# First self-attention's outputs stored head by head from SBUF, and divided by the softmax sums in the dense stage after it

## The reference, cut to what matters

```python
h1 = _ln(x, n1_g, n1_b)
q = (h1 @ q1).reshape(b, n, 20, 16).transpose(0, 2, 1, 3)     # k, v alike
sim = jnp.einsum('bhid,bhjd->bhij', q, k) * 16 ** -0.5
a = jax.nn.softmax(sim, axis=-1)
out = jnp.einsum('bhij,bhjd->bhid', a, v)
out = out.transpose(0, 2, 1, 3).reshape(b, n, 320)
x = out @ o1_w + o1_b + x
h2 = _ln(x, n2_g, n2_b)
q = h2 @ q2                                                   # queries of the cross-attention
```

## Time and profile before

| | |
|---|---|
| median of 3 runs | 3340.49 us (3337.49 to 3342.36) |
| the profiled execution | 3342.7 us, its span 3341.0 us |
| PE busy | 2936.9 us, 88% |
| DVE busy | 2157.7 us, 65% |
| ACT busy | 1892.4 us, 57% |
| POOL busy | 805.5 us, 24% |

### The profile page before, as it was taken

How to read it: one execution, slowest core, us unless ns; L and a number is a source line. 1 busy time by engine, 2 the same in 40 slices (tenths; PEclk the granted TensorE clock), 3 DMA queues, 4 the chain that set the end, 5 groups by cost and what they waited for, 6 DMA issues and landing times. The chain is left out here.

```text
span 3341.0 us, 47964 instructions
## 1 busy us (share of the span) xinstructions
PE 2936.9 (88%) x15594; PEld 1775.7 (53%) x15594; DVE 2157.7 (65%) x3834; ACT 1892.4 (57%) x3214; POOL 805.5 (24%) x1149
## 2 busy tenths in 40 slices
PE   6989999978696999998959999879978577899999
PEld 5754444457455888886731111111126342788888
DVE  5668888837453444444649999968868685444443
ACT  4328888844353232233549999989975355333322
POOL 2021221114640000000027888200003471200000
PEclk9969999989798999998975555555559898899999
DMA  8663333336762000001567557266723213010000
GB/s 228 211 166 101 106 107 103 90 80 158 165 176 46 10 10 19 9 0 38 152 173 163 128 137 164 32 90 83 97 56 96 79 45 92 26 36 18 25 17 16
DMA packets 358243, 296.57 MB, mean 89 GB/s; under 512 B 175602, under 2 KB 281914, under 8 KB 358058
## 3 DMA queue, kind: packets, MB, share of 16 engines
q1 hardware_dynamic: 347994, 273.93, 34.0%
q0 software_dynamic: 7280, 18.07, 2.1%
q10 hardware_dynamic: 2784, 2.29, 0.4%
HBM read 177.53 MB, written 114.52 MB: 87 GB/s over the span
## 5 line engine op out<-in xcount | busy, mean ns | idle before, releaser
L1591 PE MATMUL nat<-k_stack,q_stack 48*128 48x512 bf16 x640 | 381.0, 605 | 71.5 <-DMA k_stack<-k1w 31.1
L1391 DVE TENSOR_REDUCE neg_max<-nat 128x1 f32<-128x512 f32 x640 | 400.7, 682 | 61.3 <-PE nat L1250 61.2
L1625 DVE TENSOR_REDUCE m_all<-nat 128x1 f32<-128x512 f32 x640 | 423.3, 691 | 18.1 <-PE nat L1591 17.8
L804 POOL TENSOR_TENSOR rstd<-var_eps,neghalf 128x4 f32<-128x4 f32 x48 | 51.9, 1081 | 1588.0 <-DVE var_eps L1028 1588.0
L1645 ACT ACTIVATE nat<-nat,m_all 128x512 f32<-128x512 f32 x640 | 427.7, 2130 | 3.0 <-DVE m_all L1625 2.9
L1645 ACT ACTIVATION_READ_ACCUMULATOR nat<-nat,m_all 128x1 f32 x640 | 403.6, 1674 | 0.0
L1054 DVE SCALAR_TENSOR_TENSOR ff<-outp,bias,gel 128x512 f32<-128x512 f32 x160 | 120.1, 751 | 417.6 <-PE outp L326 417.6
L1325 ACT ACTIVATE probs<-sT 128x1024 f32<-128x1024 f32 x320 | 328.0, 1027 | 93.1 <-PE sT L1259 85.5
L968 ACT ACTIVATE gel<-outp,bias 128x512 f32<-128x512 f32 x160 | 110.0, 688 | 351.6 <-PE outp L326 351.6
L1839 ACT ACTIVATE exps<-sT 128x1024 f32<-128x1024 f32 x320 | 293.4, 1573 | 10.5 <-PE sT L1788 10.5
L972 ACT CAST ff_hi<-ff 128x512 fp32r<-128x512 f32 x160 | 99.2, 620 | 312.3 <-DVE ff L1054 312.3
(11 more groups left out here) (561 smaller groups left out, 7163.3 us busy)
## 6 DMA issues: line engine op xcount, KB each, us to landing
v<-vpad SPq DMA_DIRECT2D x64, 320.0 KB, 2.8
q_stack<-q_part SPq DMA_DIRECT2D x90, 160.0 KB, 5.8
k_stack<-k1w SPq DMA_DIRECT2D x90, 160.0 KB, 10.5
q_stack<-q_hi SPq DMA_DIRECT2D x160, 64.0 KB, 2.5
v_stack<-v SPq DMA_DIRECT2D x40, 256.0 KB, 3.2
q_stack<-q_hi SPq DMA_DIRECT2D x80, 128.0 KB, 2.8
raw<-v SPq DMA_DIRECT2D x16, 640.0 KB, 14.9
k_stack<-k_hi SPq DMA_DIRECT2D x158, 64.0 KB, 2.2
```

Source lines behind the costliest of these rows:

```text
L1391: dve.tensor_reduce(neg_max[:, n % 2, qt, 2 * pr + ab:2 * pr + ab + 1], nat[(16 * (n + 2) + t) % 3][:, :], AX.X, ALU.max, negate=True).the ...
L1591: pe.matmul(bank[i % NAT][:, :], q_stack[half, slot, g, pr, qt * P:(qt + 1) * P], k_stack[half, slot, g, pr, :], start=True, stop=True).th ...
L1625: dve.tensor_reduce(k.m_all[:, column(i // TILES, i % TILES)], bank[i % NAT][:, :], AX.X, ALU.max, negate=True).then_inc(s["e_max_ready"], 1)
```

## The change

**In the attention.** The outputs are no longer turned, normalised and stored by token. `turn_output` on PE, the copy `o_turned` on ACT, the reciprocal of each quad on DVE and `norm` on POOL are gone. ACT copies `o_ps` into one of two buffers `o_sb[:, n % 2]`, and POOL stores them as they are (`store`, L1379 to L1385): one DMA for the four rows of sums and one for each head's 16 rows, five a quad. POOL does this for quad m-5 in its pass m, behind the parts. ACT's copy waits for `b_o_stored{n % 2}`, that is for all five stores of the quad which last used its buffer. Once per sample SP loads the 20 rows of sums (`load_sums`), DVE inverts them (`invert`), POOL splits the result in a high and a low part (`split_shares`), SP stores both.

**In the dense stage.** It runs by feature. The `oT` transposes are gone; instead PE spreads the inverted sums of a sample to the features (`scale`, three matmuls of a 40-row matrix `spread` with the 40 rows `shares`), and DVE multiplies the loaded outputs by them in place, ahead of the split. The three steps stand behind `("stats", 0)` and are taken two samples ahead. SP loads the outputs in 3 DMAs and the shares in one.

```diff
+        scale = [("scale", m) for m in range(3)] if recips is not None else []
...
+            if scale:
+                ahead["scale"] = 2
+            body = [("stats", 0), *scale, *oT[0:2], items[0], oT[2], ("norm", 0), items[1], items[2], oproj[0], ("double", 0),
                     zT[0], zT[1], oproj[1], zT[2], oproj[2], oproj[3]]
...
                 def load_attn_T(b, split_b=None):
                     if split_b is not None:
                         sp.wait_ge(s["oT_split"], at["oT_split"] + split_b * 3 + 3)
+                    if scale:
+                        sp.dma_start(words(shares[:, :]), rows(recips, b * (2 * HEADS), 2 * HEADS)
+                                     ).then_inc(s["attn_in_loaded"], 16)
...
+                    if kind == "scale":
+                        if isinstance(b, int) and b + m == 0:
+                            pe.wait_ge(s["spread_set"], at["spread_set"] + 1)
+                        if m == 0:
+                            pe.wait_ge(s["attn_in_loaded"],
+                                       at["attn_in_loaded"] + b * (16 * n_attn) + 16 * n_attn)
+                        bank_free(pe, st, b)
+                        pe.matmul(bank_of(st, r)[:, :], spread[:, m * P:(m + 1) * P], shares[:, :], start=True, stop=True
+                                  ).then_inc(s[turned[st][0] + "_full"], 1)
+                    elif kind == "oT" and not by_feature:
...
+                    if kind == "scale":
+                        if m == 0:
+                            dve.wait_ge(s["attn_in_loaded"],
+                                        at["attn_in_loaded"] + b * (16 * n_attn) + 16 * n_attn)
+                        bank_full(dve, st, b)
+                        dve.tensor_tensor(attn[:, m, :], attn[:, m, :], bank_of(st, r)[:, :], ALU.mult
+                                          ).then_inc(s[turned[st][0] + "_drained"], 1)
...
+                def load_sums(b):
+                    for r in range(2):
+                        wait(sp, f"b_o_stored{r}", 80 * ((QUADS * (b + 1) - r + 1) // 2))
+                    sp.dma_start(sums, rows(sums_dram, b * HEADS, HEADS).rearrange("h (x t) -> h x t", t=P)
+                                 ).then_inc(s["a_sums_loaded"], 16)
+
+                def store_shares(b):
+                    wait(sp, "a_share_split", 2 * b + 2)
+                    for i, half in enumerate((share_hi, share_lo)):
+                        sp.dma_start(rows(recips, (2 * b + i) * HEADS, HEADS).rearrange("h (x t) -> h x t", t=P),
+                                     words(half)).then_inc(s["a_recip_stored"], 16)
...
+                    if exists(n - 4) and (n - 4) % QUADS == QUADS - 1:
+                        load_sums((n - 4) // QUADS)
+                    if exists(n - 7) and (n - 7) % QUADS == QUADS - 1:
+                        store_shares((n - 7) // QUADS)
...
-                def turn_output(n):
-                    wait(pe, "a_o_copied", n + 1)
-                    wait(pe, "a_turn_free", output_use(n) - 1)
-                    for qt in range(TT):
-                        mm = pe.transpose(output_bank(n)[:, qt * P:(qt + 1) * P], o_sb[:, qt * P:(qt + 1) * P],
-                                          k.ident[:, :])
-                    mm.then_inc(s["a_turn_full"], 1)
...
                         wait(act, "a_pv_done", n - 1)
-                        wait(act, "a_turn_full", output_use(n - 3) + 1 if n > 2 else 0)
-                        act.copy(o_sb[:, :], o_ps[:, :]).then_inc(s["a_o_copied"], 1)
+                        wait(act, f"b_o_stored{n % 2}", 80 * (n // 2 - 1))
+                        act.copy(o_sb[:, n % 2, :], o_ps[:, :]).then_inc(s["a_o_copied"], 1)
...
-                        if exists(n - 2) and j == 2:
-                            wait(act, "a_turn_full", output_use(n - 2) + 1)
-                            wait(act, "a_o_normed", n - 3)
-                            act.copy(o_turned[:, n % 2, :], output_bank(n - 2)).then_inc(s["a_turn_free"], 1)
...
-                def norm(n):
-                    r = n % 2
-                    wait(pool, "a_recip", n + 1)
-                    wait(pool, f"a_o_stored{r}", 16 * (n // 2))
-                    o = o_turned[:, r, :].rearrange("p (t h c) -> p t h c", t=TT, h=4)
-                    pool.tensor_tensor(o_nat[:, r], o[:, :, :, 0:DH],
-                                       recip[:, r].unsqueeze(3).broadcast_to([P, TT, 4, DH]), ALU.mult
-                                       ).then_inc(s["a_o_normed"], 1)
-                    wait(pool, "a_o_normed", n + 1)
+
+                def store(n):
+                    wait(pool, "a_o_copied", n + 1)
+                    done = s[f"b_o_stored{n % 2}"]
+                    pool.dma_start(rows(sums_dram, n * 4, 4), o_sb[DH:P:VCOL, n % 2, :]).then_inc(done, 16)
+                    for h in range(4):
+                        pool.dma_start(rows(out, (4 * n + h) * DH, DH), o_sb[VCOL * h:VCOL * h + DH, n % 2, :]
+                                       ).then_inc(done, 16)
+
+                def split_shares(b):
+                    wait(pool, "a_recip", b + 1)
+                    wait(pool, "a_recip_stored", 32 * b)
+                    pool.tensor_copy(share_hi, shares).then_inc(s["a_share_split"], 1)
+                    wait(pool, "a_share_split", 2 * b + 1)
+                    pool.tensor_tensor(share_lo, shares, share_hi.bitcast(F32), ALU.subtract
+                                       ).then_inc(s["a_share_split"], 1)
 
...
-                    if n >= 4:
-                        norm(n - 4)
+                    if n >= 5:
+                        store(n - 5)
+                    if n > 2 * QUADS and n % QUADS == 2:
+                        split_shares(n // QUADS - 2)
                     loader.turn(pool, n)
                     if n < BATCH * TT:
                         early.add(pool, n)
-                for n in range(NQ - 4, NQ):
-                    norm(n)
+                for n in range(NQ - 5, NQ):
+                    store(n)
+                for b in (BATCH - 2, BATCH - 1):
+                    split_shares(b)
 
             @block.vector
             def _(dve):
                 dve.memset(words(k_stack[0:64, 0, :, :]), 1.0).then_inc(s["a_first_set"], 1)
                 dve.memset(words(parts[:, :, :]), 0.0).then_inc(s["a_parts_set"], 1)
...
+                def invert(b):
+                    wait(dve, "a_sums_loaded", 16 * (b + 1))
+                    wait(dve, "a_share_split", 2 * b)
+                    dve.reciprocal(shares, sums).then_inc(s["a_recip"], 1)
+
+                for n in range(-2, NQ + 5):
+                    if not exists(n + 2) and exists(n - 5) and (n - 5) % QUADS == QUADS - 1:
+                        invert((n - 5) // QUADS)
```

More of the change, by code:

```diff
@@ L510, in passed @@
             self.s.passed(name, n)
+        for name in ("pool_w_loaded0", "pool_w_loaded1", "bias_loaded", "b_o_stored0", "b_o_stored1"):
+            self.s.before(name)
+        self.s.retire([name for name in self.counts if name not in ("c_loaded", "c_v_stored")
+                       and not name.startswith("c_w_loaded")])
 def dense_phase(nc, s, k, layer, main, ln_g, ln_b, ws, wo=None, attn_in=None,
                 ff_bias=None, stores=None, final=None, next_weights=(), by_feature=False, next_bias=None, load=False,
-                opening=None):
+                opening=None, recips=None, recips_stored=None):
     with ExitStack() as ctx:
@@ L551, in dense_phase @@
                 turned = {st: x for st, x in turned.items() if st[0] != "oT"}
+                turned.update({st: ("oT", st[1], 3) for st in scale})
             if not has_o:
@@ L852, in step @@
                     kind, m = st
-                    if kind == "oT" and not by_feature:
+                    if kind == "scale":
[8 more added lines that the diff above has]
+                    elif kind == "oT" and not by_feature:
                         if m == 0:
@@ L940, in step @@
                             bank_full(act, st, b)
+                        elif scale:
+                            name, count = bank_read(scale[m], b)
+                            act.wait_ge(s[name], count)
                         elif m == 0:
@@ L1117, in dense_phase, with self_attention @@
             opening.passed()
[L1120 removed]
+def self_attention(nc, s, k, q, kk, v, out, sums_dram, recips, next_weights, bias):
     RING = 5
@@ L1140, in self_attention @@
         shift_sb = sb("shift_sb", [32, 2, TOK], F32R)
-        recip = sb("recip", [P, 2, TT, 4])
-        o_sb, o_turned = sb("o_sb", [P, TOK]), sb("o_turned", [P, 2, TOK])
-        o_nat = sb("o_nat", [P, 2, TT, 4, DH])
+        o_sb = sb("o_sb", [P, 2, TOK])
+        sums, shares = (k.m_all[0:TT * HEADS, P * i:P * i + P] for i in range(2))
+        share_hi, share_lo = (k.s_all[0:TT * HEADS, P * i:P * i + P].bitcast(F32R) for i in range(2))
         loader = PoolLoader(nc, s, ctx, next_weights, 320)
@@ L1220, in _ @@
```

(4 more changed lines are left out.)

63 lines of the change are left out of this document (31 added, 32 removed).

## The result

| | us |
|---|---|
| before, median of 4 | 3341.43 (3337.49 to 3347.41) |
| after, median of 4 | 3686.14 (3680.02 to 3693.03) |
| ratio | 1.103, 95% interval 1.101 to 1.105 |
| profiled span, before and after | 3341.0 and 3691.3 |
| mean granted clock, before and after | 0.841 and 0.784 |

The account below looks back on a forecast made before the run. PE and DVE were taken to share the attention's bound. Terms 351 - 4 + 5 + 16 = +368 us on the profiled 3342.7 gave 3711, stated as 3708 us against the median; range 3560 to 3795.

Parts of the forecast that it names:

- The wait and its place: Attention: ACT's copy of quad n-2 waits in rounds 4 to 38 for same-round stores; +10.0 us a round, +351 us.
- rival 4: Attention: stores are done when ACT asks, as if the pass were mistaken by one round; 3309 to 3333 us, chance 0.05.
- The landing: Attention: the fifth store lands 3.0 us after its issue, bounds 2.1 and 4.5.
- The stretch behind the wait: Attention: from shift rows to next round 12.8 us, taken from round 1 with late clock recovery; round 21.6 us.
- rival 2: Attention: the clock never returns within a round; +12.4 us a round, 3793 us, chance 0.2.
- The price of lateness: Attention: each further microsecond of issue or landing costs 35 us.
- Rival 3: Attention: stores land late, 4.5 us instead of 3.0, +52 us; 3760 us, chance 0.07.
- The removed work: Attention: output transposes cost PE 0.76 us a round; were nothing else changed, 38 full rounds give 29 us back.
- The stage's end: Last copy to dense stage's first load: issues, landing, sums, inversion and SP issues add 5 us, bounds 0 and +9.
- The dense stage: Three more DVE steps a sample, no PE gain counted as the third scale waits; +16 us, bounds -8 and +25.
- DVE's steps: Dense stage: three more DVE steps of 128x512 at 0.69 us each, +2.07 us a sample over 8 samples.
- Signs: Expected in the changed profile: attention ending near 1060 us; dense-stage period near 17.5 us with DVE busiest.

Follow-up runs that it names:

- e1: The changed kernel, with POOL storing quad m-3 instead of m-5 in its pass m; 3357.0 us, 1.0035 of the kernel before.
- e5: The changed kernel, with POOL storing quad m-4 instead of m-5 in its pass m; 3359.1 us, 1.0045 of the kernel before.
- e3: The changed kernel, with six useless PE products ahead of the shift rows' transposes in rounds 4 to 37; 3565.2 us, 1.066 of the kernel before.
- e10: The changed kernel, with nine small POOL additions ahead of the stores in each pass; 3716.9 us, 1.114 of the kernel before.
- e2: The changed kernel, with POOL's stores and share splitting moved behind the loader's work and early bias; 3681.4 us, 1.101 of the kernel before.
- e4: e1, with the dense stage's third spread product and the splits moved behind the first query projection; 3347.0 us, 1.0009 of the kernel before.
- e11: e4, with DVE's dense-stage multiplication done for one column instead of 512, pricing only; 3339.0 us, 0.9993 of the kernel before.
- e6: e1, with the third multiplication and next sample's z ahead of the oT_lo subtractions, and z's transposes ahead of projections; 3348.3 us, 1.0022 of the kernel before.
- e12: e6, with POOL's casts of the next stage's weights held back until DVE has done z and oT_lo; 3329.6 us, 0.9961 of the kernel before.

## Why the prediction was right, and where it was off

**The wait and its place: right.** The copy of quad n-2 waits in 35 rounds for stores issued in the same round; e1 and e5 show that one pass makes all of it, and rival 4's point of decision (the wait vanishes if the pass is mistaken by one round) is what they ran. Their 3357 and 3359 us lie above rival 4's 3309 to 3333, since the stage's end and the dense stage cost more than it allowed.

**The landing: too long by 1.1 us.** Step by step against a round that starts at 579.31: first issue after 2.06 us (forecast 2.07), fifth after 4.10 (4.2), copy after 5.97 (7.19), shift rows after 7.63 (8.8). Issues are 0.60 us for the sums and 0.48 for each head (0.53 taken). The error is the landing: the copy goes on 1.9 us after the fifth issue begins, where I took 3.0 from the nearest of POOL's rows, an 80 KB load. SP's 2.1, my lower end, was the nearer one. The fit of the Trainium skill (DMA: Bandwidth & Descriptors, Anatomy of one DMA — SWDGE (gpsimd) path) gave 2.1 by estimate. The trace agrees, with a median of 2.1; by it the forecast would have been 3677.

**The stretch behind the wait: the number right, in part by luck.** 12.82 us against 12.8, taken from round 1. The clock fell in each of the 35 pauses and came back once in every round, so rival 2 did not occur. But round 1 stood at the low clock from the stage's beginning, and nothing in the rows of the kernel before told how long the low clock lasts behind a pause: that the first 9.5 us of the stretch were low there and here alike is coincidence. e3 prices the low clock at 4.1 us a round. The Trainium skill (TensorE: Matmul & The Clock Gate, HAM oscillation) has each burst behind a wait start cold. The trace agrees: 0.50 behind each pause.

**The price of lateness: too high.** Rival 3 counted 35 us a microsecond; e10 shows 28 by the medians (30.8 by 1.10) and 20 by the profiled executions, e2 nothing for 0.6.

**The removed work: right.** -27.9 us (e1) and -26.0 (e5) against -29.

**The stage's end: +9.8 for +5.** The chain of copy, stores, sums, inversion and shares ran from 1004.02 to the end of the last issue at 1013.6, 9.6 us, the lower end of what I had added up. The 5.6 us from there to the load were not in the sum, and the upper bound of +9 did not hold them.

**The dense stage: +28.8 for +16, above the bound of +25.** I saw that the third `scale` waits for a bank, and used it only to deny PE a gain. It is a wait in PE's own stream with everything queued behind it, and it takes the clock down: moving it (e4) gives 7.8 us. DVE's steps, the +16.6 of my sum, gave 5.9 to 7.5. I also priced `oT_lo` at its old 0.69, though the diff puts its operand from PSUM to SBUF. In the change itself that cost little: one of a sample's three subtractions lies beside POOL's work, 3.5 us in all, and z gave back 7.0 (453 ns for 672), because it had moved clear of it. It counts once the order is mended, as e11 and e6 show. e11, with PE's step moved and DVE's steps nearly out, takes 15.3 us off e1's seven periods; the 13.6 that it leaves match the 14.1 us by which z and `oT_lo` are slower in it, but no run takes out these two alone.

**Signs.** The stage was to end near 1060 us, which does not follow from the sum (some 1044 for the last copy) and was 1019. In the dense stage the mean period is 19.5 us, not 17.5, and PE, not DVE, is busiest (118.8 us against 101.9 from 1030 to 1180).

The sum of 368 was thus made of an attention 39 us too dear and the rest 22 us too cheap, 4 of them behind the dense stage, where I had counted nothing. That the forecast lay only 22 us, 0.6%, above the median owes something to these errors going against each other.

## What to carry to other kernels

When stores are counted in passes of one engine and buffers in rounds of another, write down in which round each store is issued and in which its buffer is wanted: here one index between 5 and 4 was worth 327 us, of which about two fifths was the clock that fell in the pauses (e3: 121 us by the medians, 134 by the profiled executions). Ahead of an in-order queue ask of every new instruction what frees its bank and what stands behind it. And when an operand moves from PSUM to SBUF, look at what GpSimd does at that time before you take the old duration.

## What was unexpected on the chip

- The low clock lasted 13.6 us from its fall in the rounds read of three kernels, with pauses of PE of 5.5, 6.2 and 6.7 us, though PE was busy for the last 8.3 to 9.5 us of it. In e2's early rounds it was 6.8 or 10.2 us.
- Beside POOL's casts a subtraction of 128x512 with both operands in SBUF took 1298 ns in the mean, 684 without them. The same casts lie beside z in the kernel before (672 ns; 441 in e12), so holding them back may help that kernel too; that was not tried.
- A store of POOL with 16 partitions of 2 KB holds it 0.48 us and lands 2.1 us in the median (1.7 to 2.9) after its issue; in e2 and e10 the median is 1.8.
